# Graph attention with residual and norm: the scores' target rows spread over the partitions by DMA instead of TensorE, counts kept in 16 bits

## What is computed

```
h = (x @ W).reshape(n, H, C)
alpha_s = jnp.einsum('nhc,hc->nh', h, a_s)
alpha_d = jnp.einsum('nhc,hc->nh', h, a_d)
e = jax.nn.leaky_relu(alpha_s[src] + alpha_d[dst], 0.2)
m = jax.ops.segment_max(e, dst, num_segments=n)
e = jnp.exp(e - m[dst])
denom = jax.ops.segment_sum(e, dst, num_segments=n)
alpha = e / (denom[dst] + 1e-16)
out = jax.ops.segment_sum(h[src] * alpha[:, :, None], dst, num_segments=n)
...
h = elu(gat_layer(x, W1, ..., concat=True))      # 512 x 6144
x = layernorm(x + gat_layer(h, W2, ...))         # 512 x 768
```

## Time and profile before

| | before |
|---|---|
| median of 3 runs | 641.99 us (641.72 to 642.11) |
| the profiled execution: its time | 641.79 us |
| its span from first to last instruction | 640.0 us |
| PE busy | 632.6 us, 99% of the span |
| DVE busy | 529.6 us, 83% |
| ACT busy | 336.3 us, 53% |
| POOL busy | 208.1 us, 33% |
| DMA | 28.2% of 16 engines' span |

### The profile page before, as it was taken

The page is one execution under the profiler, slowest core; times in us unless marked ns, Lnnn a source line. Parts: engine busy times, 40 slices in busy tenths (PEclk is TensorE's granted clock), DMA queues, the critical chain, the costliest instruction groups (busy, mean ns, idle before and its releaser), DMA issues.

```text
span 640.0 us, 9306 instructions
## 1 busy us (share of the span) xinstructions
PE 632.6 (99%) x3426; PEld 543.9 (85%) x3426; DVE 529.6 (83%) x928; ACT 336.3 (53%) x570; POOL 208.1 (33%) x122
## 2 busy tenths in 40 slices
PE   9999999999999999999999999999999999999996
PEld 5766568989888898989899988999898989887885
DVE  8999997889989878758684858797689868789876
ACT  7899982546524645444353635363455344534382
POOL 1000000140743824067404940375207540451230
PEclk9999999999999999999999999999999999999999
DMA  8422503125144323042302520270307130500002
GB/s 317 161 75 75 160 15 99 50 54 194 51 147 146 127 99 99 1 153 95 100 1 72 175 59 16 75 227 23 97 20 237 65 100 5 192 26 1 1 2 99
DMA packets 22173, 59.36 MB, mean 93 GB/s; under 512 B 2544, under 2 KB 2800, under 8 KB 22128
## 3 DMA queue, kind: packets, MB, share of 16 engines
q1 hardware_dynamic: 21984, 58.69, 28.2%
q10 hardware_dynamic: 144, 0.07, 0.0%
HBM read 54.03 MB, written 4.72 MB: 92 GB/s over the span
## 4 chain that ended last, share of the span: by engine, by line
PE 89%; DVE 9%; issue 0%; ACT 0%; DMA 0%; ACTq 0%
PE O L1289 31%; PE R L1184 9%; PE R L1190 9%; PE R L1187 9%; PE R L1256 6%; PE R L1262 6%; PE R L1259 6%; DVE ohd L709 3%; PE O L1201 3%; DVE ohs L713 2%; PE R L1206 1%; DVE junk L749 1%; PE O L1256 1%; PE O L1262 1%; PE O L1259 1%; PE O L1434 1%
## 5 line engine op out<-in xcount | busy, mean ns | idle before, releaser
L1111 POOL TENSOR_TENSOR W2l<-Wr,W2h 128x768 fp32r<-128x768 f32 x48 | 92.6, 1948 | 126.1 <-ACT W2h L425 126.1
L1184 PE MATMUL R<-W1h,xTh 128*128 128x384 f32 x312 | 106.3, 341 | 0.0
L1115 POOL TENSOR_TENSOR Pl<-L,Ph 128x512 fp32r<-128x512 f32 x34 | 55.5, 1651 | 153.8 <-ACT Ph L474 153.6
L1187 PE MATMUL R<-W1l,xTh 128*128 128x384 f32 x312 | 105.4, 338 | 0.0
L1190 PE MATMUL R<-W1h,xTl 128*128 128x384 f32 x312 | 105.4, 338 | 0.0
L1105 POOL TENSOR_TENSOR W1l<-Wr,W1h 128x768 fp32r<-128x768 f32 x30 | 58.8, 1970 | 129.3 <-ACT W1h L414 128.9
L749 DVE CUSTOM_DVE_ANT_0 junk<-h,abc 128x768 bf16<-128x768 f32 x64 | 64.0, 999 | 27.8 <-ACT h L437 26.7
L1289 PE MATMUL O<-W2h,gh 128*128 128x256 f32 (+1 forms) x384 | 78.5, 339 | 0.0
L1289 PE MATMUL O<-W2h,gl 128*128 128x256 f32 (+1 forms) x384 | 77.4, 336 | 0.0
L1289 PE MATMUL O<-W2l,gh 128*128 128x256 f32 (+1 forms) x384 | 77.4, 336 | 0.0
L1256 PE MATMUL R<-Ph,hh 128*128 128x512 f32 x168 | 66.3, 395 | 0.0
(11 more groups left out here) (186 smaller groups left out, 1186.2 us busy)
## 6 DMA issues: line engine op xcount, KB each, us to landing
Wr<-in_W SPq DMA_DIRECT2D x101, 384.0 KB, 3.6
abc<-in_as SPq DMA_DIRECT2D x9, 384.0 KB, 5.5
abc<-in_ad SPq DMA_DIRECT2D x9, 384.0 KB, 5.3
h_rows<-h SPq DMA_DIRECT2D x8, 384.0 KB, 2.4
hl<-h_rows SPq DMA_DIRECT2D x8, 384.0 KB, 6.0
xin<-in_xT SPq DMA_DIRECT2D x6, 256.0 KB, 5.8
xr<-in_x SPq DMA_DIRECT2D x1, 1536.0 KB, 6.7
out<-res SPq DMA_DIRECT2D x4, 384.0 KB, 2.3
```

Source lines behind the costliest of these rows:

```text
L1111: e.tensor_tensor(W2l[:, m % N2, :], Wr[:, n, :], W2h[:, m % N2, :].bitcast(f32), ALU.subtract).then_inc(s_w2l, 1)
L1115: e.tensor_tensor(Pl[:, t, d0:d1], L[:, t, d0:d1], Ph[:, t, d0:d1].bitcast(f32), ALU.subtract).then_inc(s_Pl, 1)
L1184: e.matmul(bank[:, 0:HALF], xTh[:, f, xs], hi[:, ws], start=f == 0, stop=False)
L1187: e.matmul(bank[:, 0:HALF], xTh[:, f, xs], lo[:, ws], start=False, stop=False)
```

## The change

- The list LOADS, SP's program, ACT's program and POOL's program put the piece w2(h-1,5) behind all of w1(h+1) in heads 3 to 6 (before it stood behind w1(h+1,1) in the loads, and ahead of w1(h+1,2) on ACT and POOL).
- CT is kept in 16-bit integers, and a tile `rows` (two rows of 512 f32 on each partition) takes the room.
- For heads 1 to 6 SP stores r12 to DRAM (`store_rows`, one element after the other: 1024 of 4 bytes in heads 1 and 2, 512 in heads 3 to 6), waits until the store has landed, and reads rows of 2 KB back onto all 128 partitions (`spread_rows`): two rows in heads 1 and 2, only ACT's row in heads 3 to 6.
- TensorE's transposes of those rows are gone: 8 in head 1, 8 in head 2, 4 in each of heads 3 to 6. DVE's row of heads 3 to 6 is still transposed. Heads 0 and 7 and the second layer keep both.
- In heads 3 to 6 ACT casts w1(h+1,2..4) ahead of the scores, w1(h+1,5) at tile 1 and w2(h-1,5) at tile 2.
- The first product of stage C is no longer cut in two parts, since banks O2 and O3 hold no rows of head 1.

```diff
@@ the order of the banks
     RING += [("as", 2, 0), ("den", 1, 0)] + [("A", 1, c) for c in range(FT)]
-    RING += [("r2", 2, 0), ("r1", 2, 0)]
     for h in range(EARLY, H + 1):
...
         if h < H:
-            RING += [("B", h, n) for n in range(4, 8)] + [("as", h, 0), ("r2", h, 0), ("r1", h, 0)]
+            RING += [("B", h, n) for n in range(4, 8)] + [("as", h, 0)]
+        if h < H:
+            RING += [("r2", h, 0) for _ in range(1) if h == H - 1] + [("r1", h, 0)]
@@ tiles
-        CT = sb("CT", [128, NT, N], f32)
+        CT = sb("CT", [128, NT, N], u16)
+        rows = sb("rows", [128, 2, N], f32)
...
+        tr = nc.dram_tensor("t_rows", (H, 2 * N), f32, kind="Internal").ap()
...
+        def row_ready(h, i):
+
+            return ((s_tr1, s_tr2)[i % 2], 16 * h) if 0 < h < (EARLY if i == 2 else H - 1) else bc_value(h, i)
+
+        def row_bank(h, i):
+            return rows[:, 2 - i, :] if 0 < h < (EARLY if i == 2 else H - 1) else ring_bank(("r2", "r1")[i - 1], h, 0)
@@ SP
+            def store_rows(h):
+                e.wait_ge(s_r12, 2 * h + 2)
+                with nc.allow_non_contiguous_dma(reason="columns to rows"):
+                    lo = 0 if h < EARLY else 1
+                    e.dma_start(tr[h, lo * N:2 * N].rearrange("(i t p) -> p i t", i=2 - lo, t=NT), r12[:, lo:2, :]).then_inc(s_ts, 16)
+
+            def spread_rows(h):
+
+                e.wait_ge(s_ts, 16 * h)
+                if h > 1:
+                    e.wait_ge(s_L, NT * h)
+                    e.wait_ge(s_lk, NT * h)
+                e.dma_start(rows[:, 1, :], tr[h:h + 1, N:2 * N].broadcast_to([128, N])).then_inc(s_tr2, 16)
+                if h < EARLY:
+                    e.dma_start(rows[:, 0, :], tr[h:h + 1, 0:N].broadcast_to([128, N])).then_inc(s_tr1, 16)
...
                 if h + 1 < H:
-                    for k in range(2, FT):
-                        load_raw("w1", h + 1, k)
+                    load_raw("w1", h + 1, 3)
+                    load_raw("w1", h + 1, 4)
+                    store_rows(h)
+                    load_raw("w1", h + 1, 5)
+                    spread_rows(h)
+                load_raw("w2", h - 1, 5)
@@ ACT, heads 3 to 7
                     high_w2(h - 1, 4)
-                    high_w2(h - 1, 5)
-                    scores(h, h, 0, NT, ring_bank("r2", h, 0), (gl_value(h - 1, FT - 1), (s_g, FT * h)), 3 * h + 2,
-                           lambda u, h=h: high_w1(h + 1, 1 + u) if h + 1 < H and 1 <= u <= 4 else None)
+                    if h + 1 < H:
+                        for k in range(2, 5):
+                            high_w1(h + 1, k)
+
+                    def last_rows(u, h=h):
+                        if u == 1 and h + 1 < H:
+                            high_w1(h + 1, 5)
+                        if u == 2:
+                            high_w2(h - 1, 5)
+                    scores(h, h, 0, NT, row_bank(h, 1), (gl_value(h - 1, FT - 1), (s_g, FT * h)), row_ready(h, 1), last_rows)
@@ DVE, maxima
+                if 1 < h < H:
+
+                    e.wait_ge(s_ts, 16 * (h - 1))
                 e.tensor_tensor(r12[:, 0, lo:hi], ad, mc[:, lo:hi], ALU.subtract).then_inc(s_r12, 1)
@@ POOL
                     low_w2(h - 1, 4)
-                    low_w2(h - 1, 5)
                     if h + 1 < H:
                         for k in range(2, FT):
                             low_w1(h + 1, k)
+                    low_w2(h - 1, 5)
@@ TensorE
-                if n == 5:
-                    e.wait_ge(s_y, 2)
-                    targets(1, 0, NT, (ring_bank("r2", 1, 0), ring_bank("r1", 1, 0)), 4)
...
-                    if c == (0 if h == 2 else 1 if h == H - 1 else 2) and h > 1:
-                        targets(h, 0, NT, (None, None), 2 * h + 2)
+                    if c == (1 if h == H - 1 else 2) and h >= EARLY:
+                        targets(h, 0, NT, (None, None) if h == H - 1 else (None,), 2 * h + 2)
```

More of the change, by code:

```diff
@@ L40, in gat_resnorm_kernel @@
         LOADS += [("w2", h - 1, k) for k in range(4)] + [("v", H - 1, k) for k in V_ROWS.get(h, ())]
-        LOADS += [("w2", h - 1, 4)] + [("w1", h + 1, k) for k in range(2) if h + 1 < H]
-        LOADS += [("w2", h - 1, 5)] + [("v", H - 1, k) for k in V_SCORES.get(h, ())]
-        LOADS += [("w1", h + 1, k) for k in range(2, FT) if h + 1 < H]
+        LOADS += [("w1", h + 1, k) for k in range(2) if h + 1 < H] + [("w2", h - 1, 4)]
+        LOADS += [("w1", h + 1, 2) for _ in range(1) if h + 1 < H] + [("v", H - 1, k) for k in V_SCORES.get(h, ())]
+        LOADS += [("w1", h + 1, k) for k in range(3, FT) if h + 1 < H] + [("w2", h - 1, 5)]
     LOADS += [("w2", H - 1, k) for k in range(FT)]
@@ L323, in sync_program @@
             load_raw("w2", 1, 1)
+            store_rows(1)
             store_h(2, 1)
             load_raw("w2", 1, 2)
+            spread_rows(1)
             reload_h(1)
@@ L333, in sync_program @@
                 load_raw("w1", 3, k)
-            for k in range(N2, FT):
-                load_raw("w2", 1, k)
+            load_raw("w2", 1, 4)
+            store_rows(2)
+            load_raw("w2", 1, 5)
+            spread_rows(2)
             load_raw("w1", 3, 3)
@@ L350, in sync_program @@
                     load_raw("w1", h + 1, 1)
-                load_raw("w2", h - 1, 5)
+                load_raw("w2", h - 1, 4)
+                if h + 1 < H:
+                    load_raw("w1", h + 1, 2)
                 if h + 3 == H:
@@ L461, in scores @@
                         if u == 0:
-                            e.wait_ge(s_bc, bc)
+                            e.wait_ge(*bc)
                             e.wait_ge(s_as02, h + 1)
@@ L549, in head_2 @@
                     evict_B(2, 0, u // 2 - 1)
-            scores(0, 0, 0, NT, ring_bank("r2", 0, 0), (), 2, head_2)
+            scores(0, 0, 0, NT, row_bank(0, 1), (), row_ready(0, 1), head_2)
             evict_B(2, 1, 0)
@@ L562, in head_2 @@
                             evict_B(2, 3, u // 2 - 1)
-                    scores(1, 1, 0, NT, ring_bank("r2", 1, 0), (gl_value(0, FT - 1), (s_g, FT)), 5, head_2)
+                    scores(1, 1, 0, NT, row_bank(1, 1), (gl_value(0, FT - 1), (s_g, FT)), row_ready(1, 1), head_2)
                     high_sums(1)
@@ L576, in scalar_program @@
                     scaled_as(2, 24)
-                    scores(2, 2, 0, NT, ring_bank("r2", 2, 0), (gl_value(1, FT - 1), (s_g, 2 * FT)), 8, lambda u: high_w1(3, 3 + u) if u in (1, 2) else None)
+                    scores(2, 2, 0, NT, row_bank(2, 1), (gl_value(1, FT - 1), (s_g, 2 * FT)), row_ready(2, 1), lambda u: high_w1(3, 3 + u) if u in (1, 2) else None)
                     high_h(2, 0)
@@ L680, in scalar_program @@
             scaled_as(H, 65)
-            scores(H, H, 0, NT, ring_bank("r2", H, 0), (gl_value(H - 1, FT - 1), (s_g, FT * H)), 26, first_h2)
+            scores(H, H, 0, NT, row_bank(H, 1), (gl_value(H - 1, FT - 1), (s_g, FT * H)), row_ready(H, 1), first_h2)
             part_h2(2, 1, 3)
@@ L782, in maxima @@
                     if t == 0:
-                        e.wait_ge(s_bc, 3 * h + 1)
+                        e.wait_ge(*bc_value(h, 0))
                         if h >= EARLY:
@@ L932, in vector_program @@
             sums_h(1, 3, h32[:, 1, :], abc[:, 1, :, :])
-            scores(0, 0, 0, NT, ring_bank("r1", 0, 0), 3)
+            scores(0, 0, 0, NT, row_bank(0, 2), row_ready(0, 2))
             e.wait_ge(s_sd, 2)
@@ L958, in vector_program @@
                     sums_2(2)
-                    scores(1, 1, 0, NT, ring_bank("r1", 1, 0), 6)
+                    scores(1, 1, 0, NT, row_bank(1, 2), row_ready(1, 2))
                     sums_P(1, lambda: sums_2(3))
@@ L964, in vector_program @@
                 if h == 2:
-                    scores(2, 2, 0, NT, ring_bank("r1", 2, 0), 9)
+                    scores(2, 2, 0, NT, row_bank(2, 2), row_ready(2, 2))
                     sums_P(2, lambda: low_h(2, 0))
@@ L983, in vector_program @@
                         products_W2(k, 0 if i else 8 * h + 8)
-                    scores(h, h, 0, NT, ring_bank("r1", h, 0), 3 * h + 3)
+                    scores(h, h, 0, NT, row_bank(h, 2), row_ready(h, 2))
                     sums_P(h)
@@ L1034, in vector_program @@
             maxima(H, 0, NT, ring_bank("as", H, 0))
-            scores(H, H, 0, NT, ring_bank("r1", H, 0), 27)
+            scores(H, H, 0, NT, row_bank(H, 2), row_ready(H, 2))
             for t in range(NT):
@@ L1217, in targets @@
                 e.wait_ge(s_r12, ready)
-                for i, bank in zip((1, 0), banks):
+                for i, bank in zip((1, 0)[2 - len(banks):], banks):
                     if bank is None:
@@ L1361, in tensor_program @@
                         half_B(h, n // 2, n % 2, take("B", h, n))
-                if h == 1:
-                    for c in range(2):
-                        stage_C(0, c, groups=range(4), ends=False)
-                    for c in range(2):
-                        stage_C(0, c, groups=(4, 5))
```

(2 more changed lines are left out.)

11 lines of the change are left out of this document (8 added, 3 removed).

## The result

The changed kernel takes 695.61 us in the median of 4 runs (695.28 to 697.78), the kernel before 642.05: ratio 1.084, 95% interval 1.082 to 1.087. The profiled execution took 697.78 us, with a span of 696.0, 56.0 more than before. The forecast was 648.0 us with a range of 638.5 to 656.0: the sign was right and the size was wrong by 48 us.

What follows compares the result with a forecast made beforehand. PE, busy 632.6 of 640.0 us, was taken as the bound. Terms -3.5 + 6.2 + 2.8 + 0.5 = +6.0 us on the profiled 641.79 gave 647.8, stated as 648.0, range 638.5 to 656.0.

Steps and rivals of the forecast that it cites:

- What each row costs now: Heads 1 to 6: store, landing wait and read through DRAM take 5.5 us from r12 to SBUF, bounds 4.2 and 7.7.
- What is removed: 32 transposes of 0.11 us each leave PE in heads 1 to 6: 3.5 us, the whole gain.
- When r12 is ready: POOL's unbroken subtractions delay DVE's small instructions: r12 at 283.7 (282.8 to 284.6) in heads 3, 4; 281.2 in 5, 6.
- When PE needs it: First score step must start by 286.06; rows 3.1 us late each in heads 3, 4, 1.4 each in 5, 6.
- Heads 1 and 2: DVE's L814 reads r1 from SBUF beside POOL: 0.5 us lost in head 2, nothing taken in head 1.
- At nothing: ACT's row reads from SBUF (0.03 us each, hidden), 16-bit CT and SP's ten more DMAs cost nothing.
- Rival (c): Single-element store takes 6 us or more instead of 2.4, adding 3.6 us in each of four heads: 662; 7 in 100.

Runs made afterwards that it cites:

- experiment 4: Changed kernel with ACT's last W1h cast ahead of the scores in heads 3 to 6: 697.05 us; separately, changed kernel with 32 overwritten filler matmuls on PE: 703.05 us.

## Why the prediction was wrong

The failed step is "What each row costs now", with "the nearest for the store is h_rows with 2.4 us": the trip through DRAM was taken at 5.5 us, and it measured 14.8 in head 3, of which 9.5 were the store, 3.2 with one piece per partition. The range fell with it: its upper bound for store and read, 7.7 us, was taken from other forms of transfer. The read was short as well: 3.0 us, against 5.3 in head 3 and 4.1 to 4.9 behind the short store. The interpolation by size went below the 5.3 us of abc, the one load of the same form, and the page of before has six loads of 256 KB (xin) at 5.8 us. The sign didn't hang on the store: with the short one the kernel is still 17.9 us slower than before. The rest by its own steps:

- **What is removed.** Right. 32 fewer matmuls on PE, and in the kernel with the trip in heads 1 and 2 alone 16 fewer, of which 1.25 of 1.76 us show at head 3.
- **When r12 is ready.** Right in its mechanism: zm, mc and both r wait for POOL in heads 3 and 4. The second r was blocked as well (1.84 us), so r12 was there 0.8 us later than the middle I took and near the late end, 284.6 (290.52 less the 6.04 us that heads 1 and 2 had cost is 284.5, against 283.7). For heads 5 and 6 it was right to the tenth: in head 5 zm took 1.87 us, mc 1.77 and both r 0.16, and r12 was there 7.0 us behind the source rows (452.75 - 445.76), as in 281.2 - 274.2. The 282.3 given for PE at the transposes of r1 doesn't fit, which has 282.90; with that the wait is up to 1.7 us, and it measured 1.6. It is no term of the sum. In the kernel with the new order alone this costs what the waits show, 1.6 us in each of the two heads.
- **When PE needs it.** Right in size: 8.6 us were forecast from the first score step to the end of the fourth L814, now L866; from 305.39 to 313.83 it is 8.44. The sum for head 3, with measured terms, is 3.1 + 0.8 (r12) + 7.1 (store) + 2.3 (read) = 13.3 us late. The excess of the head over the forecast's 67.93 us (68.37 of the chain before, less the four transposes) is 83.23 - 67.93 = 15.3. The other 2.0 is about what the slow clock adds behind the last wait: from 313.88 to 318.77 fifteen matmuls take 4.9 us, where fifteen at 0.17 would take 2.6. That share is read from rows and no run undid it. For heads 5 and 6 the forecast had 1.4 us each, with DVE's four products of W2 as the last to end. In head 5 they ended at 459.75 and the rows came at 466.05; the two heads took 9.9 and 10.8 us longer than before. This is the step of the trip again, not one of their own.
- **Missed.** The cast of W1h(h+1,5) behind the rows (no cost of its own, experiment 4), and the granted clock that falls with PE's waits. A forecast that has PE idle for several microseconds at a place should ask this, and mine didn't.
- **Heads 1 and 2.** Wrong for head 1, at "I take nothing", and with it "At nothing", where SP "waits most of the time" and only the loads behind the read were looked at. I looked at what the four VectorE instructions cost, and not at what stands in SP's queue behind the wait for the store, though SP's issues were part of the change. It cost most of the 6.0 us by which head 3 began late; with the short store head 3 began 1.25 us early. L866 from SBUF did meet POOL (744 to 2347 ns in heads 1 and 2, a median of 779), as forecast for L814, and PE waited 0.3 us for the eviction of h in head 2, where 0.5 was forecast.
- **Rival (c)** named the cause, single elements that are dear, and gave it 7 in 100 with the argument "only 32 for each of 16 engines". Its price was too low as well (6 us or more, 662 in all). What should have raised it was in the text already: no row of before was near a store of 4-byte pieces, and the Trainium skill, "DMA: Bandwidth & Descriptors", section "Rules for kernel authors", advises against exactly this form. One descriptor for each element is what the trace bears out (27516 packets against 24188 with one piece per partition: 3328 more, which is 4096 elements less 768 pieces). The advice is borne out by the times of neighbours (128 of them 8.2 us) and not by those of elements that stand apart (64 bytes apart 1.4 us).

In all, 695.6 - 641.9 = 53.7 us part as follows by the runs: the counts 0; the order 4.9; the trip with a short store, in that order, 13.1 more (659.8 - 646.7); single elements in place of short pieces 35.8 more.

## What to carry to other kernels

A transfer whose form the trace of before doesn't show should not be priced by the nearest one that differs in form; the size alone doesn't give it (4 KB took 1.4 or 9.3 us here by the layout alone), and the upper bound must be open. Before a wait is put into a queue, list what stands behind it: here one wait on SP held up a reload that had nothing to do with it by 10.8 us, and head 3 began 6.0 us late. And when a supply comes late, its place among the other duties of the engine that uses it decides how much else comes late with it: with the same short trip the kernel took 669.1 us in the order that has four casts of W1 behind the rows, and 659.8 in the order that has one.

## What the runs showed of the hardware

- A store of 4-byte elements that are neighbours in DRAM (up to 128, one from each partition): 64 elements 8.5 us, 128 8.2 to 8.4, 256 9.3, 512 8.1 to 11.9, 1024 9.3 and 10.8; but 32 take 3.0, 16 take 1.35. In the changed kernel 512 took 8.4 to 9.5. Spaced 8, 16, 32, 64, 128 and 512 bytes apart, 512 elements take 4.4, 2.9, 2.4, 2.4, 2.2 and 1.8 us. 128 pieces of 16 bytes take 1.4 to 2.6. In the lone store of 512 neighbours the trace shows no packet after the first 2 us; what is long is the time until the landing is reported.
- A VectorE instruction of 128 x 4 numbers with both inputs in SBUF takes as long as the GpSimd subtraction beside it: four in a row took 1.87, 1.78, 1.78 and 1.84 us, where alone they take 0.16.
- Reading an SBUF row with a stride of four values (16 bytes) costs ScalarE 1.22 us instead of 0.72 for 512 columns, and VectorE's operation on two SBUF inputs 1.15 instead of 0.78 in the median, with GpSimd at work in part of them.
- The granted clock of PE stood at 1.00 while it was idle from 302 to 305 and at 0.50 from 305 on, by stretches; with dense matmuls from 313.9 it was back at 1.00 from 319. In the kernel before it was 1.00 throughout these heads.
